# An expert phase with two sum tables in place of three, one reciprocal root for two row units, and three of its shared units moved behind the experts

## The reference, cut to what matters

```python
Xp = x[slots_token].reshape(E, C, d)
G = jnp.einsum('ecd,edi->eci', Xp, W_gate)
U = jnp.einsum('ecd,edi->eci', Xp, W_up)
Y = jnp.einsum('eci,eid->ecd', jax.nn.silu(G) * U, W_down)
Yf = Y.reshape(EC, d) * slots_w[:, None]
out = jnp.zeros((T, d), x.dtype).at[slots_token].add(Yf)
shared = jax.nn.silu(x @ shared_gate.T) * (x @ shared_up.T) @ shared_down.T
return (out + shared).reshape(b, s, d)
...
x = _layernorm(x + _L1_ffn_ref(x, ...), axis=-1)
```

## Time and profile before

| | us |
|---|---|
| median of 3 runs | 2076.2 (2076.19 to 2076.82) |
| the profiled execution | 2070.69 |
| its span in the trace | 2068.9 |
| busy in the span: PE / DVE / ACT / POOL | 1905.4 / 1569.4 / 1050.2 / 848.5 |

### The profile page before, as it was taken

The page is one execution under the profiler, slowest core; times in us unless marked ns, Lnnn a source line. Parts: engine busy times, 40 slices in busy tenths (PEclk is TensorE's granted clock), DMA queues, the critical chain, the costliest instruction groups (busy, mean ns, idle before and its releaser), DMA issues. The chain is left out here.

```text
span 2068.9 us, 36884 instructions
## 1 busy us (share of the span) xinstructions
PE 1905.4 (92%) x12560; PEld 1711.4 (83%) x12560; DVE 1569.4 (76%) x4310; ACT 1050.2 (51%) x2677; POOL 848.5 (41%) x877
## 2 busy tenths in 40 slices
PE   7999999999999969999799999999999999978960
PEld 6788888888888858887689999999999999868960
DVE  8977878787887655565578888888888888855647
ACT  5434333343333233332477766666666666625753
POOL 2232223223232310000244566566666666554767
PEclk9999999999999979999799999999999999998985
DMA  3200000010000224743000010000000000107868
GB/s 123 82 1 31 21 11 32 1 31 11 21 21 1 74 92 131 264 163 112 19 12 16 27 37 21 21 23 20 18 18 19 18 13 29 60 18 194 197 124 301
DMA packets 108890, 125.64 MB, mean 61 GB/s; under 512 B 12727, under 2 KB 100731, under 8 KB 108064
## 3 DMA queue, kind: packets, MB, share of 16 engines
q1 hardware_dynamic: 91632, 110.96, 16.7%
q0 software_dynamic: 12288, 8.11, 2.6%
q10 hardware_dynamic: 4784, 4.21, 0.6%
HBM read 79.48 MB, written 59.85 MB: 67 GB/s over the span
## 5 line engine op out<-in xcount | busy, mean ns | idle before, releaser
L237 POOL TENSOR_TENSOR rwkv_gate<-rwkv_key,rwkv_gate 128x512 f32<-128x512 f32 x128 | 204.1, 1595 | 524.6 <-DVE rwkv_key L442 524.6
L1413 POOL TENSOR_TENSOR kept_raw<-kept_raw,mla_row_inv 128x512 f32<-128x512 f32 x192 | 199.2, 1038 | 302.0 <-DVE mla_row_inv L1765 300.8
L310 ACT ACTIVATE rwkv_gate<-rwkv_r 128x512 f32<-128x512 f32 x128 | 76.6, 598 | 400.6 <-DVE rwkv_o_low L363 398.1
L1570 ACT ACTIVATE kept_raw<-kept_raw,mla_least 128x256 f32<-128x256 f32 (+1 forms) x512 | 227.9, 446 | 90.9 <-DVE mla_least L1749 89.8
L1749 DVE CUSTOM_DVE_ANT_0 kept_raw<-mla_score,kept_mask 128x256 f32<-128x256 f32 (+1 forms) x512 | 156.9, 352 | 79.8 <-PE mla_score L2124 79.4
L427 DVE TENSOR_TENSOR rwkv_kv<-rwkv_v,rwkv_key 128x512 f32<-128x512 f32 x128 | 88.1, 688 | 124.9 <-PE rwkv_v L475 122.6
L434 DVE TENSOR_TENSOR_SCAN rwkv_state<-rwkv_decay_w,rwkv_kv 128x256 f32<-128x256 f32 x256 | 166.2, 691 | 4.1
L2124 PE MATMUL mla_score<-mla_k_high,mla_q_high 128*128 128x256 f32 (+1 forms) x512 | 155.6, 304 | 0.0
L492 PE MATMUL rwkv_out<-rwkv_w_high,rwkv_o_high 128*128 128x256 f32 x512 | 144.1, 281 | 5.7 <-DVE rwkv_o_low L363 5.7
L492 PE MATMUL rwkv_out<-rwkv_w_high,rwkv_o_low 128*128 128x256 f32 x512 | 145.3, 284 | 0.0
L492 PE MATMUL rwkv_out<-rwkv_w_low,rwkv_o_high 128*128 128x256 f32 x512 | 144.3, 282 | 0.0
(11 more groups left out here) (402 smaller groups left out, 6427.2 us busy)
## 6 DMA issues: line engine op xcount, KB each, us to landing
moe_y_in<-sums SPq DMA_DIRECT2D x48, 256.0 KB, 4.8
sums<-ffn_empty SPq DMA_DIRECT2D x21, 512.0 KB, 7.6
kept_raw<-in_experts SPq DMA_DIRECT2D x27, 384.0 KB, 4.9
kept_raw<-in_rkvo SPq DMA_DIRECT2D x16, 512.0 KB, 3.3
slots<-ffn_empty SPq DMA_DIRECT2D x8, 722.5 KB, 6.6
moe_e_rows<-slots SPq DMA_DIRECT2D x32, 180.6 KB, 3.8
kept_x_in<-x SPq DMA_DIRECT2D x18, 256.0 KB, 2.6
mla_x_res<-x SPq DMA_DIRECT2D x17, 256.0 KB, 2.9
```

What stands on the lines that cost most here:

```text
L237: nc.gpsimd.tensor_tensor(gate[:, c % 2, :], key[:, c % 2, :], gate[:, c % 2, :], ALU.mult).then_inc(gated_done, 1)
L1413: nc.gpsimd.tensor_tensor(unit, unit, row_inv[:, v % PR, 0:len(heads)].rearrange("p (h a) -> p h a", a=1) .to_broadcast([P, len(heads), ke ...
L1570: last = nc.scalar.activation(probs[:, v % PR, i * keys:(i + 1) * keys], masked[:, v % 2, i * keys:(i + 1) * keys], ACT.Exp, bias=least[:, ...
```

## The change

Six edits, all but the last two in `moe_phase`:

- Two sum tables. Both halves of an expert go to table `e % 2`, and POOL waits, before the first half of expert `e`, for both halves of expert `e - 2`; between the two halves it waits for nothing. The tail loads and adds two tables for a unit.
- The ring of loaded sums holds 6 units (the same memory as 4 units of three tables).
- Reciprocal root, variance and shift are taken for two units at once (`GROUPS`): seven pairs, then the last two units singly. POOL has two more `add_first` done before it waits for a pair's variance.
- Shared units are dealt out one for each four experts (`PACE` 4). Seven (`INSIDE`) run inside the experts, three in a loop of their own behind the last expert. On DVE that loop stands before `combine(0, 0)`.
- The shared gate of unit 0 comes after `expert_out(0)`, not before it.
- `ffn_phase` clears two sum tables, which are 128 rows longer, and gives the two halves of an expert different spare rows, by two DMAs for a piece of `slots` in place of one.

```diff
-SUMS = 3
-SUMROWS = TOKENS + P
+SUMS = 2
+SUMROWS = TOKENS + 2 * P
...
-SUMRING = 4
+SUMRING = 6
 OUTRING = 4
-PACE = 3
+PACE = 4
 LATE = UNITS - EARLY
+PAIRS = (UNITS - 2) // 2
+GROUPS = [(2 * g, 2) for g in range(PAIRS)] + [(UNITS - 2, 1), (UNITS - 1, 1)]
+INSIDE = 7
...
             def add_rows(e):
                 pool.wait_ge(y_copied, e + 1)
+                if e >= SUMS:
+                    for a in range(2):
+                        pool.wait_ge(y_added[(e - SUMS) % RING][a], 16 * ((e - SUMS) // RING + 1))
                 for a in range(2):
-                    if 2 * e + a >= SUMS:
-                        e1, a1 = divmod(2 * e + a - SUMS, 2)
-                        pool.wait_ge(y_added[e1 % RING][a1], 16 * (e1 // RING + 1))
                     nc.gpsimd.indirect_dma_start(
-                        sums_dram[(2 * e + a) % SUMS],
+                        sums_dram[e % SUMS],
...
-            add_first(0)
-            for n in range(UNITS):
-                if n + 1 < UNITS:
-                    add_first(n + 1)
-                rsqrt(n)
+            added = 0
+            for g, (first, units) in enumerate(GROUPS):
+                while added < min(first + units + (2 if g < PAIRS - 1 else 1), UNITS):
+                    add_first(added)
+                    added += 1
+                rsqrt(g)
...
-                if piece == 2 and u < LATE:
+                if piece == 2 and u < INSIDE:
                     shared_low(u)
...
+            for u in range(INSIDE, LATE):
+                if u > INSIDE:
+                    add_shared(u - 1)
+                if u + 1 < LATE:
+                    x_low(u + 1)
+                shared_hidden(u)
+                shared_low(u)
+            add_shared(LATE - 1)
...
+            for g, (first, units) in enumerate(GROUPS):
+                for n in range(first, first + units):
+                    combine(g, n)
+                variance(g)
+                if g > 0:
+                    shift_mean(g - 1)
+            shift_mean(len(GROUPS) - 1)
...
                 if e == 0:
-                    shared_gate(0)
                     expert_out(0)
...
+            for u in range(INSIDE, LATE):
+                shared_gate(u)
+                if u > INSIDE:
+                    shared_out(u - 1)
+                if u + 1 < LATE:
+                    turn_x(u + 1)
+                shared_up(u)
+            shared_out(LATE - 1)
```

More of the change, by code:

```diff
@@ L2591, in apply_norm @@
                 act.dma_start(unit_rows(out, n), x_out[:, n % OUTRING, :, :]).then_inc(stored[n % OUTRING], 16)
[L2593 to L2594 removed]
+            for g, (first, units) in enumerate(GROUPS):
+                for n in range(first, first + units):
+                    apply_norm(g, n)
         @block.vector
@@ new lines, in variance @@
+            def variance(g):
+                first, units = GROUPS[g]
+                if g >= 2:
+                    dve.wait_ge(normed, GROUPS[g - 1][0])
+                dve.wait_ge(counted, UT * (first + units))
+                for t in range(units * UT):
+                    last = nc.vector.bn_aggr(moments[:, g % 2, t, :], stats[:, g % 2, t, :])
+                last.then_inc(stats_done, 1)
+                dve.wait_ge(stats_done, g + 1)
+                nc.vector.tensor_scalar(var_eps[:, g % 2, 0:units * UT], moments[:, g % 2, 0:units * UT, 1], LN_EPS, None,
+                                        ALU.add).then_inc(var_done, 1)
@@ new lines, in shift_mean @@
+            def shift_mean(g):
+                w = GROUPS[g][1] * UT
+                dve.wait_ge(rstd_done, g + 1)
+                nc.vector.scalar_tensor_tensor(shift[:, g % 2, 0:w], moments[:, g % 2, 0:w, 0], -1.0,
+                                               rstd[:, g % 2, 0:w], ALU.mult, ALU.mult).then_inc(shifted, 1)
+            for g, (first, units) in enumerate(GROUPS):
+                for n in range(first, first + units):
+                    combine(g, n)
+                variance(g)
+                if g > 0:
+                    shift_mean(g - 1)
```

99 lines of the change are left out of this document (44 added, 55 removed).

## The result

| | before | after |
|---|---|---|
| median, us | 2076.19 (2074.21 to 2076.88, 6 runs) | 2064.64 (2063.18 to 2069.67, 6 runs) |
| the profiled execution | 2070.69 | 2063.18 |
| its span | 2068.9 | 2061.0 |

The ratio is 0.9953, 95% interval 0.9943 to 0.9963. That is 9.8 us by the ratio and 11.6 us by the two medians, and not the 21.6 that were forecast.

What follows compares the result with a forecast made beforehand. PE was taken to pace the experts, with DVE, POOL and DMA engines all full in the tail. DVE free at 2007.5 plus 39.8 gave a span of 2047.3 against 2068.9, −21.6 us: median 2054.6, range 2048 to 2064.

Steps and rivals of the forecast that it cites:

- Three units out of the experts: Experts: removing 120 shared matmuls saves 13.6 us of PE's time, of which 2.7 us are given back.
- ACT takes over in such a step, by 0.3 us: Expert steps without shared matmuls: PE needs 2.5 us, ACT 2.8; nine more such steps give back 2.7 us.
- The start: First expert output no longer behind the first shared gate: POOL starts some 3 us earlier, PE saves about 1 us.
- Three units behind the experts: Loop behind the last expert: hand-overs between engines lie bare, 18.2 us, so DVE is free at 2007.5.
- The scatter: Indirect DMAs into the sum tables: POOL just keeps up; their end is hidden by the shared units, by 2.9 us.
- the scatter sets the end: Rival, 12%: indirect DMAs land in 6 us on the mean, an expert takes 4.25 us; time 2065.
- two halves on one table hinder each other: Rival, 4% on the slower side: DMA halves queue on a table, landing 8 us, an expert 5.25; time 2096.
- The tail: From DVE's free moment to the end: 31.5 us of cycles, 7.2 and 1.1 for the end, 39.8 us.
- it runs two units ahead and hides that: Tail: POOL's 3.8 us a pair, 4.1 with a hand-over, is hidden; at most 1.4 us more if not.
- So DVE sets the cycle: Tail: DVE, not POOL or the DMA engines, sets 3.9 us a pair and 2.1 a single unit.
- the full sum of both engines: Port rival, 2%: POOL and DVE exclusive in the tail, 3.9 us a unit, tail 62 us, time 2085.
- The clock: Rival, 8%: PE's clock falls in the loop behind the experts; 13.1 us in full, 2067.7, or partly 2057 to 2062.

Runs made afterwards that it cites:

- ACT's order: Changed kernel with ACT taking the high part of expert e + 2's weights before the copy of expert e - 1's results; 2058.57 us, ratio 0.9925.
- all ten inside: Changed kernel with all ten shared units inside the experts, one for three experts, and no loop behind them; 2060.31 us, ratio 0.9936.
- single roots: Changed kernel with root, variance and shift taken for each unit singly instead of for pairs; 2067.57 us, ratio 0.9963.
- the gate first: Changed kernel with the first shared gate ahead of the first expert's output again, on PE and ACT; 2067.48 us, ratio 0.9977.
- adds shared: Changed kernel with DVE doing both table additions of units 3, 7 and 11; 2064.66 us, ratio 0.9962.
- the kernel before with two tables: Kernel before plus only the two tables, POOL's wait for both halves of e - 2, ring of 6 and the clearing; 2065.66 us, ratio 0.9961.
- ten units inside with ACT's order and shared adds: Changed kernel with all ten shared units inside, ACT's weights before its copy, and DVE doing both table additions of units 3, 7, 11; 2057.40 us, ratio 0.9926.

## Why the prediction was wrong

Counted from the phase's start the forecast was 184.0 us (2047.3 − 1863.3), and 195.4 were measured, 11.4 more. In its own steps:

**Three units out of the experts: 8.4 us too much.** The failed step is "ACT takes over in such a step, by 0.3 us", and with it the 2.7 us given back. It priced a bare step by the busiest engine, 2.8 us. The step is a loop of latencies over ACT and DVE, 3.45 to 3.49 us, and ACT's order shows it: one instruction out of the loop, and it takes 2.91. The kernel before shows it too, in the timeline of ACT, from copy to copy:

```profile
1905.10 0.81 ACT L2547 ACTIVATE moe_y_rows<-moe_y,moe_e_rows 80x256 f32<-80x256 f32 x2
...
1909.18 0.81 ACT L2547 ACTIVATE moe_y_rows<-moe_y,moe_e_rows 80x256 f32<-80x256 f32 x2
...
1913.72 0.82 ACT L2547 ACTIVATE moe_y_rows<-moe_y,moe_e_rows 80x256 f32<-80x256 f32 x2
...
1917.17 0.82 ACT L2547 ACTIVATE moe_y_rows<-moe_y,moe_e_rows 80x256 f32<-80x256 f32 x2
```

These steps of 4.08, 4.54 and 3.45 us are a group of three, so a unit inside cost 12.07 − 3 × 3.45 = 1.7 us, not 40 × 0.1136 = 4.5. In the changed kernel's groups of four (15.8 to 15.9 us) it costs 2.0: ten units at 1.7 and seven at 2.0 differ by 3 us. PE was 19.93 of 20 us busy, yet its matmuls of the shared units mostly filled time that the loop left. The forecast was 10.9 for three units; 2.5 came.

**The start: 2.4 us too little.** Costed at 1.0 ("saves PE only the idle time that is now filled"), measured at 3.4, and 3.9 when undone. A loop of latencies that starts 3.4 us earlier ends 3.4 us earlier; only work of a full PE would not.

**Three units behind the experts: right.** 18.2 forecast (the terms as they are listed add up to 18.5), 18.9 from the end of the last expert matmul (1997.73) to 2016.67. The size of the loss was right, and it is larger than what it buys: all ten inside is at least as fast.

**The scatter: right.** It is hidden by 3.4 us (forecast 2.9). The landings did not lengthen enough to bind; the rivals in which the scatter sets the end, or two halves on one table hinder each other, did not come.

**The tail: 4.6 us too little.** 39.8 forecast, 44.4 measured. The failed step is "it runs two units ahead and hides that", and "So DVE sets the cycle". POOL's additions and root are a sum that no running ahead hides: 2.88 + 1.46 + 0.08 = 4.42 us a pair, where 3.9 was forecast and 4.1 held possible (2.2 us in six cycles). And that sum is longer than the forecast's 3.8 because DVE stops POOL in it. The timelines of DVE and POOL at the end of the changed kernel show POOL's addition and its root of two columns, each first behind an addition of DVE and then without one:

```profile
2044.72 0.67 DVE L2697 TENSOR_TENSOR moe_total<-moe_y_in,moe_total 128x512 f32<-128x512 f32 x1
2044.88 1.67 POOL L2480 TENSOR_TENSOR moe_total<-moe_y_in,moe_total 128x512 f32<-128x512 f32 x1
...
2048.39 1.27 POOL L2480 TENSOR_TENSOR moe_total<-moe_y_in,moe_total 128x512 f32<-128x512 f32 x1
...
2050.13 0.68 DVE L2697 TENSOR_TENSOR moe_total<-moe_y_in,moe_total 128x512 f32<-128x512 f32 x1
2050.23 1.15 POOL L2486 TENSOR_TENSOR moe_rstd<-moe_var_eps,moe_minus_half 128x2 f32<-128x2 f32 x1 [0.57 <-DVE moe_var_eps L2713]
...
2053.50 0.70 POOL L2486 TENSOR_TENSOR moe_rstd<-moe_var_eps,moe_minus_half 128x2 f32<-128x2 f32 x1 [2.12 <-DVE moe_var_eps L2713]
```

Beside no addition of DVE POOL's addition takes 1.27 us and the root of two columns 0.70. Begun while DVE adds, they take 1.67 and 1.15: the time until DVE's addition ends, and 1.14 and 0.57 us more. So some 0.4 us for one of a pair's two additions and, if the root of four columns loses as much as that of two, some 0.45 for its root are waiting that the rows count as busy. The prediction threw this out ("The rows disagree for these instructions", "cannot be exclusive"). It read 18.52 and 18.09 busy of 20 us as work side by side; but DVE's statistics run beside POOL's additions, and the two engines' additions do not. The rival it priced was the full sum of both engines, 62 us of tail, and that did not come; a part of it did. (The sum of the tail also counts 7.2 us for the 7.4 that the text reads behind the last variance.)

 The last two units come 3.28 us apart and not 2.1 (2.4 us): DVE may not start a group's variance until ACT has used the root and shift of the group before last, whose places it takes, and ACT is late, since a pair's two outputs reach it at once. The timeline of DVE at the end:

```profile
2049.70 0.25 DVE L2710 BATCH_NORM_AGGREGATE moe_moments<-moe_stats 128x2 f32<-128x6 f32 x2 [1.37 <-ACT moe_x_out L2598]
...
2052.97 0.25 DVE L2710 BATCH_NORM_AGGREGATE moe_moments<-moe_stats 128x2 f32<-128x6 f32 x2 [1.37 <-ACT moe_x_out L2598]
```

The second could have been seen: the wait stands in the code. Of the first, gives 2 × 1.33 + 1.11 = 3.8; a root of four columns (1.46, for which the forecast had 1.11) was in no row of before, and how the additions would fall against DVE's wasn't either.

**The clock.** In this profile it held at 1.00 behind the experts, in the stretch where the rival put its fall (1998 to 2017: 1.00). In three others it did fall there, to 0.50 under the last unit's matmuls (2019 to 2021 with single roots and with the gate first, 2017 to 2019 with adds shared). From the last expert matmul to the last shared addition these took 21.2, 19.4 and 20.8 us for 18.9, a part of it, in the first and the last, the delayed `moe_h_low`. And it fell where no rival looked, in the bare steps of the experts, in some executions. It isn't in the first profile, so it explains nothing of the 11.4 us, but it is a likely cause of the changed kernel's spread (2061.2 to 2069.7), while ACT's order stayed within 2058.1 and 2059.0 in five executions of one series. "TensorE: Matmul & The Clock Gate" of the Trainium skill, Part 1, has the clock halved unless recent activity holds it up; these traces agree, and show that bare steps of one kind fall on either side of it.

**The sum.** −8.4 + 2.4 − 0.7 − 4.6 = −11.3 against the forecast, of the 11.4 measured. Of the 10.2 us gained, the kernel before with two tables has 5.8, and the start 3.4 to 3.9; pairs give 2.1 in the tail, and the three units behind the experts give back what taking them out gained. The parts were each measured in another surrounding, and add up to a little more than the whole.

**A better version.** Of all kernels, ten units inside with ACT's order and shared adds has the lowest median (2057.40, 0.9926) and the changed kernel with ACT's order alone the lowest ratio (0.9925); their intervals overlap. Both beat the changed kernel (0.9953) by about 6 us. The order of two lines on ACT is enough for that with seven units inside. With ten inside it shows nothing beyond the noise (0.9934, and 0.9936 without it), since PE bounds those groups.

## What to carry to other kernels

A busy engine in a stretch with mixed steps is not proof that it sets the pace: look at the step with the least of its work, walk from one instruction to the same one in the next step, and price what is taken out by the difference between steps with it and without, here 1.7 us and not 4.5. In a cycle over two engines sum each engine's whole share, waits of program order included, before saying which hides behind which. Busy time can hold waiting: take one instruction where its neighbour engine is idle and where it isn't, and compare their lengths (here 1.27 and 1.67 us, 0.70 and 1.15) before you conclude from two full engines that they work side by side. Work that leaves an engine with gaps may cost clock too, so what fills the gaps is not free to remove.

## What the runs showed of the hardware

- POOL's power of a [128 × n] tile, begun just behind an addition of DVE, takes 1.18 us for 2 columns, 1.46 for 4 and 2.10 for 8: about 0.87 us and 0.15 for each column. Some 0.45 of it is the wait: with DVE idle, as at the end of every kernel here, 2 columns take 0.70.
- POOL's additions and some instructions of DVE exclude each other, whichever starts first. `moe_var_eps` on DVE takes 0.17 us when POOL doesn't add, 0.65 in the runs with single roots and two tables, 1.08 in the changed kernel. The timeline of DVE there, and that of POOL:

```profile
2033.43 1.08 DVE L2713 TENSOR_SCALAR moe_var_eps<-moe_moments 128x4 f32<-128x4 f32 x1
...
2031.60 2.88 POOL L2480 TENSOR_TENSOR moe_total<-moe_y_in,moe_total 128x512 f32<-128x512 f32 x2
```

It ends at 2034.51, and POOL's additions at 2034.48. Over all fourteen profiles: 69 of 69 `moe_var_eps` that start amid a POOL addition end 0.02 to 0.03 us after it. 31 of 31 DVE instructions with two inputs in SBUF (table additions, and `moe_h_low`) that do end 0.55 to 0.62 us after it, one lasting up to 1.78 us for 0.68. And 97 of 97 POOL additions that start amid DVE's addition end 1.12 to 1.18 us after that. Not held up are the statistics on DVE, and its additions and products with one input in PSUM (12 cases, all 0.69 us). "SBUF — State Buffer" of the Trainium skill, Terms, has DVE and POOL share a port that one locks for a full instruction. These rows agree for the first three kinds, and show which instructions of DVE go on beside POOL's; that the cause is this port no run here shows. `moe_var_eps` costs nothing as long as POOL sets the cycle, since the root waits for POOL's additions anyway.
- One indirect DMA costs POOL 1.40 us and 0.30 between two, which is a floor of 109 us for 64; with everything else shortened, that is what the experts meet next.
